# Context rows of a perceiver layer loaded in groups of four tiles instead of two

## The reference, cut to what matters

```python
x = x + xattn(layernorm(x), ctx_768)        # cross attention, one head, E = 512
x = x + attn(layernorm(x))                  # self attention, 16 heads, relative positions
x = x + ffn(layernorm(x))                   # ternary weights, gelu

# xattn, the part that the change touches
x2 = layernorm(ctx_768, ln2_g, ln2_b)       # over the 384 columns of each of 16 x 1601 rows
scores = (x1 @ Wq + bq) @ (x2 @ Wk + bk).T * E ** -0.5
out = softmax(scores) @ (x2 @ Wv + bv) @ Wo + bo
```

## Time and profile before

| | us |
|---|---|
| median of 3 runs | 593.91 |
| lowest, highest | 593.52, 597.63 |
| the profiled execution | 593.65 |
| its span, first to last instruction | 591.9 |
| PE busy | 561.1 (95%) |
| DVE busy | 418.5 (71%) |
| POOL busy | 199.6 (34%) |
| ACT busy | 216.8 (37%) |

### The profile page before, as it was taken

How to read it: one execution, slowest core, us unless ns; L and a number is a source line. 1 busy time by engine, 2 the same in 40 slices (tenths; PEclk the granted TensorE clock), 3 DMA queues, 4 the chain that set the end, 5 groups by cost and what they waited for, 6 DMA issues and landing times.

```text
span 591.9 us, 13163 instructions
## 1 busy us (share of the span) xinstructions
PE 561.1 (95%) x5237; PEld 352.9 (60%) x5237; DVE 418.5 (71%) x1026; ACT 216.8 (37%) x513; POOL 199.6 (34%) x259
## 2 busy tenths in 40 slices
PE   8999979999999999989996899999999999999797
PEld 7654444545455454534784675957759587595654
DVE  3987579999999999846868762926639265492743
ACT  0321142546455542413123361524516245152502
POOL 0324549899989987840000100101001010010010
PEclk9999999999999999999996999999999999999999
DMA  7990689999999999937743203030120401203000
GB/s 280 374 366 3 251 297 380 343 324 316 394 368 394 360 368 384 378 113 260 266 107 102 78 19 91 19 109 20 56 52 20 107 21 72 54 3 107 20 18 19
DMA packets 58973, 108.26 MB, mean 183 GB/s; under 512 B 19984, under 2 KB 22560, under 8 KB 56864
## 3 DMA queue, kind: packets, MB, share of 16 engines
q1 hardware_dynamic: 58912, 107.41, 52.3%
HBM read 96.91 MB, written 10.49 MB: 181 GB/s over the span
## 4 chain that ended last, share of the span: by engine, by line
PE 62%; DVE 17%; DMA 8%; SPq 5%; issue 4%; POOL 3%; ACT 2%; DVEq 0%; POOLq 0%
PE u_ps L1056 9%; DVE area L1206 6%; PE u_ps L915 6%; PE bank L1033 5%; PE max_ps L1033 5%; PE s_ps L889 4%; PE max_ps L961 4%; PE bank L1079 4%; PE bank L1102 4%; PE bank L961 4%; DMA area<-in_ctx_dram 4%; PE bank L945 3%; DMA area<-in_L_xattn_Wo_dram 3%; DVE area L1215 2%; DVE area L1210 2%
## 5 line engine op out<-in xcount | busy, mean ns | idle before, releaser
L499 POOL TENSOR_SCALAR area<-area 128x384 f32<-128x384 f32 (+1 forms) x160 | 106.8, 680 | 10.3 <-POOL area L492 10.3
L1206 DVE BATCH_NORM_STATS2 area<-area 128x6 f32<-128x384 f32 (+1 forms) x208 | 104.0, 542 | 6.9 <-DMA area<-in_ctx_dram 6.8
L492 POOL TENSOR_TENSOR area<-area,minus_half 128x4 f32<-128x4 f32 (+1 forms) x56 | 60.3, 1077 | 51.1 <-DVE area L1215 49.7
L915 PE MATMUL u_ps<-area,yT_all 128*64 128x384 f32 (+1 forms) x416 | 75.9, 496 | 0.0
L545 POOL TENSOR_TENSOR area<-area,minus_half 128x1 f32<-128x1 f32 x8 | 4.4, 550 | 184.9 <-DVE area L1487 184.9
L889 PE MATMUL s_ps<-area 128*64 128x512 f32 x288 | 66.0, 593 | 0.0
L1056 PE MATMUL u_ps<-area 128*128 128x512 f16 x256 | 60.1, 379 | 0.0
L915 PEld LDWEIGHTS u_ps<-area,yT_all 128*64 128x64 f32 (+1 forms) x416 | 26.3, 136 | 29.0 <-issue 27.9
L889 PEld LDWEIGHTS s_ps<-area 128*64 128x64 f32 x288 | 20.4, 137 | 36.5 <-issue 35.5
L714 ACT CAST area<-max_ps 128x512 f16<-128x512 f32 x8 | 4.7, 586 | 97.3 <-PE max_ps L1112 97.3
L1056 PEld LDWEIGHTS u_ps<-area 128*128 128x128 f16 x256 | 24.4, 98 | 25.1 <-issue 0.6
(11 more groups left out here) (187 smaller groups left out, 1041.0 us busy)
## 6 DMA issues: line engine op xcount, KB each, us to landing
area<-in_ctx_dram SPq DMA_DIRECT2D x96, 384.0 KB, 7.1
area<-in_ctx_turned_dram SPq DMA_DIRECT2D x32, 768.0 KB, 8.2
area<-in_L_ffn_W_turned_dram SPq DMA_DIRECT2D x16, 1024.0 KB, 8.9
skew<-area SPq DMA_DIRECT2D x8, 1024.0 KB, 4.0
area<-skew SPq DMA_DIRECT2D x16, 256.0 KB, 4.4
x_sb<-in_x_dram SPq DMA_DIRECT2D x8, 256.0 KB, 8.5
out_dram<-area SPq DMA_DIRECT2D x8, 256.0 KB, 2.0
area<-in_ctx_dram SPq DMA_DIRECT2D x16, 97.5 KB
```

What stands on the lines that cost most here:

```text
L492: pool.tensor_tensor(rs[b][:, sl], ve[b][:, sl], minus_half[:, 0:n], ALU.pow).then_inc(s["rstd_ready"], 1)
L499: pool.tensor_scalar(raw[b][0:m, u, j, :], raw[b][0:m, u, j, :], negmu[b][0:m, i:i + 1], rs[b][0:m, i:i + 1], ALU.add, ALU.mult).then_inc( ...
L915: ins = pe.matmul(u_ps[u * L:(u + 1) * L, 0:DC], pT[0:m, j % NSLOT, u * L:(u + 1) * L], raw[b][0:m, u, j, :], start=(j == 0), stop=(j == N ...
L1206: dve.bn_stats(st[b][0:m, stat_at(u, j), :], raw[b][0:m, u, j, :]).then_inc(s["key_stats_done"], 1)
```

## The change

From pair 2 on, `load_next` issues nothing at an even k below 6. At k = 1, 3 and 5 it waits for four tiles of pair p - 2 (the last of them is tile 2k + 1) and loads four tiles, 2k - 2 to 2k + 1, with one DMA of 768 KB for each sequence. The tail tile is loaded as before, at k = 6. `stats` waits for the group of four at j = 0, 4 and 8, and for the tail at j = 12. Pairs 0 and 1 are loaded and waited for as before, and the other DMAs keep their places in SP's order. Each group of four counts on the semaphore of its odd k.

```diff
             def load_next(p, k):
 
-                sp.wait_ge(s["tile_weighted"], NJ * (p - 2) + min(2 * k + 2, NJ))
-                load_pair(p, k)
+                b = p % 2
+                if k == NL - 1:
+                    sp.wait_ge(s["tile_weighted"], NJ * (p - 1))
+                    load_pair(p, k)
+                elif k % 2:
+                    sp.wait_ge(s["tile_weighted"], NJ * (p - 2) + 2 * k + 2)
+                    for u in range(2):
+                        full = ctx_in[2 * p + u, 0:FT * P, :].rearrange("(p j) d -> p j d", j=FT)
+                        sp.dma_start(raw[b][:, u, 2 * k - 2:2 * k + 2, :], full[:, 2 * k - 2:2 * k + 2, :]).then_inc(raw_loaded[b][k], 16)
...
-                if j % 2 == 0:
+                if j % 2 == 0 and (p < 2 or j == FT):
                     dve.wait_ge(raw_loaded[b][j // 2], 32 * (p // 2 + 1))
+                elif j % 4 == 0:
+                    dve.wait_ge(raw_loaded[b][j // 2 + 1], 32 * (p // 2 + 1))
```

## The result

The changed kernel takes 610.42 us (median of 4 runs, 607.85 to 613.61), the kernel before beside it 595.00 (4 runs). The ratio is 1.0257, 95% interval 1.0193 to 1.0321: slower by 15 us, where the forecast was 6.4 and its range 595.0 to 607.5. The profiled execution has a span of 606.1 us against 591.9.

A forecast was written before the change was run, and what follows sets the result against it. With PE, DVE, POOL and DMA level, the prediction added 1.6 us (pair 2), 4.0 (tiles 8 to 11 of pairs 3 to 6) and 0.8 (pair 7): +6.4 on 593.65 gives 600.0, range 595 to 607.5.

The forecast's parts named there:

- What bounds the kernel: In one pair's pass PE, DVE, POOL and DMA run level; relieving one gains nothing, an added wait has little room.
- Tiles 4 to 7: Margin from issue to need 7.3 us against 6.4 to load: cost 0, or about 1 behind a weight piece.
- Pair 2: First group lands 3.6 to 4.6 us late, 1.4 hidden by POOL's addition: cost 1.6 us, ends 0.5 and 3.
- Tiles 8 to 11: Pairs 3 to 6: 1.4 us of wait less 0.5 of room in POOL, taken as 1.0 a pair, 4.0 us.
- Tiles 0 to 3 of pairs 3 to 6: DVE stops 2.0 to 3.1 us before tile 0, hidden behind POOL's bias addition: cost 0.
- the cover: POOL's bias addition holds DVE at line 1215 for 2.70 us instead of 0.2 anyway, hiding the wait before tile 0.
- Pair 7: Four tiles of DVE work follow the last landing instead of two; 0.8 us counted for the group's late landing.
- the covers fail: Rival, chance 0.17: rows come 8 to 10 us after issue, 2.0 us more in each of five pairs, 610.
- Longer packets: Rival, chance 0.07 (under 593): grouped loads move at 426 GB/s instead of 396, gaining 5.0 us, 588.6.
- the packets stay as they are: Rival, inside the forecast's 0.50: longer rows are cut as before, each of 18 groups costs 0.3 us more, 602.
- 25 us of waits: Sign: DVE's waits for context rows grow from 6.8 us to some 25.
- one microsecond a pass: Sign: the passes of pairs 3 to 6 are longer by about 1 us each in PE's sums.

The follow-up runs named there:

- from_pair3: The changed kernel, but pair 2 is still loaded by twos: 608.03 us, ratio 1.0221 to the kernel before.
- g2_only: The kernel before, with only tiles 8 to 11 loaded as one group from pair 2 on: 604.88 us, ratio 1.0156.
- g0_only: The kernel before, with only tiles 0 to 3 loaded as one group from pair 2 on: 602.48 us, ratio 1.0123.
- small_weights: The changed kernel with four feed-forward weight pieces of pairs 4 and 5 loaded by a quarter: 608.32 us, ratio 1.0213 to the kernel before.
- to_pair6: The changed kernel, but pair 7 is again loaded by twos: 606.38 us, ratio 1.0197 to the kernel before.
- g1_only: The kernel before, with only tiles 4 to 7 loaded as one group from pair 2 on: 594.71 us, ratio 1.0000.
- tiles4_7_weights_last: The kernel before, with two attention weights moved behind the last context loads and only tiles 4 to 7 loaded as a group: 592.15 us, ratio 0.9943.
- coarse_wait: The kernel before, loads by twos and as early, but DVE waits for four tiles at a time in pairs 2 to 7: 604.29 us, ratio 1.0157.

## Why the prediction was wrong

**What bounds the kernel** held. PE, DVE and POOL run level, and the waits on DVE came through: its waits for rows grew from 6.8 to 28.6 us, and PE's waits for POOL from 4.0 to 15.0.

**Tiles 4 to 7** held: 0 predicted, ratio 1.0000 alone.

**Pair 2** held: 1.6 predicted, 2.6 - 1.0 = 1.6 in the table, about 2 by `from_pair3`. The wait was 3.94, within 3.6 to 4.6.

**Two steps failed: the wait before tile 8 was priced too low, and the wait before tile 0 was put at nothing.** Alone, the groups of tiles 8 to 11 cost 9.3 us (`g2_only`) where the prediction's terms for them come to 4.8, and those of tiles 0 to 3 cost 7.3 us (`g0_only`) where its terms come to 1.6. The two steps, in this order:

**Tiles 8 to 11.** The prediction took 1.4 us of wait, less 0.5 of room in POOL, for four pairs, and counted 4.0. Three parts of it were off. The group took 6.7 to 7.6 us from issue to use and not 6.4, so that the waits were 1.73, 1.54, 2.54 and 1.63 in pairs 3 to 6. The same wait in pair 2, 1.38, was left out. And the 0.5 us of room did not show: between the third and the seventh pair's issue the waits before tile 8 in `g2_only` add up to 2.76 + 2.83 + 1.06 + 2.35 = 9.0 us. Less the 2.05 us that DVE waited in these passes before, and with the 1.9 us by which the bias additions held it longer (11.3 instead of 9.4), that gives 8.8 us, and the passes are 8.5 us longer than before. POOL had that gap before its power, but DVE, which does the rest of the pass in order, had none.

**Tiles 0 to 3 of pairs 3 to 6.** The size of the wait was off, the cover was there. The prediction worked out 2.0 to 3.1 us from pair 4 and applied it to all. Pair 4 was right by itself (7.7 us from issue to use against 6.4 to 7.5), but in pairs 5 and 6 the group took 10.4 and 9.4 us, because more than the turned chunk stood in the queue: the weight pieces issued at 169.50 and 198.44 landed 9.6 and 10.1 us later, after the groups' own issues at 178.73 and 207.72. `small_weights` shows that this is what made them late. The waits of 4.29 and 2.35 us were longer than the cover there, which was 2.73 and 1.62 us before. The cover worked: line 1215 held DVE for 2.37, 2.70, 2.73 and 1.62 us in pairs 3 to 6 before, 9.4 in all, and line 1224 for 0.78, 1.26, 0.17 and 0.34 after, 2.6 in all.

With this the four passes can be added up from DVE's side: waits of 9.96 before tile 0 (pairs 3 to 6) and 7.19 before tile 8 (pairs 2 to 5), less 2.05 that it waited there before, less 9.4 - 2.6 = 6.8 of cover, gives 8.3 us. Measured are 8.9. The prediction had 3.0 for them, the tiles 8 of pairs 3 to 5. Of the 8.3, tile 8 gives 6.0 (7.19 less 1.19 that DVE waited before the tail tile of pair 5) and tile 0 gives 2.3 (9.96 less 0.86 before tile 2 of pair 6, less 6.8).

**Pair 7** was too small as well. It was right that four tiles of work would follow the last group. But the group landed 9.9 us after its issue, at 264.1. The prediction had named the late issue and priced it at 0.8; the weight and the turned chunk ahead of the group it did not reckon. The wait of 5.16 before tile 8 replaced 2.52 and 1.64; 2.5 us were added after pair 7's first issue, and `to_pair6` puts the pair at about 3.6. The prediction had 0.8, and 1.0 for pair 6's tile 8.

**The rival "the covers fail"** gave 610, and that is where the time came out, but not by its mechanism. Rows 8 to 10 us after the issue did come, in pairs 5 and 6. But it had 2 us uncovered before each tile 0, where the four passes show 2.3 in all, and most of the time came from tile 8, which it left at the forecast's price. **"Longer packets"** gain nothing, by `g1_only` and `tiles4_7_weights_last`, and "the packets stay as they are" is excluded by the packet counts. Of the signs given in advance, 25 us of waits (28.6), the shrinking line 1224 and no wait before tile 4 were right; one microsecond a pass was not (1.8, 1.8, 3.4 and 1.9). A sign of being wrong that it had named came up as well: more than 2 us of new idle time of PE in a pass, 2.8 in the third of the four passes and 2.1 in the fourth.

The rule of the Trainium skill (DMA: Bandwidth & Descriptors, section Bandwidth) that DMAs be batched to 1 MiB and more does not help here: going from 384 to 768 KB costs nothing where it can be hidden (ratio 1.0000) and brings nothing. The figures of that section, and the fit that the prediction worked out 11.6 and 7.6 us from, are given there for DMAs issued from GpSimd; the loads here are issued by SP.

What stays open: why `coarse_wait` costs 9 us, more than its waits less the cover give. In the four passes the waits are 11.7 us; less 2.1 that were there before and 7.1 of cover they give 2.5, where 3.4 are measured. Pair 2 adds 1.4 us and the end of the stage 1.1, together 5.9, which is within the expectation. Of the 9.5 us by which its span is longer, 1.9 stand there before pair 2 is touched (the turned chunk in front of pair 2's first group is issued at 92.86 before and at 94.72), and 1.7 come after the stage, where no context is loaded. No run shows where these come from. Other profiles have such parts too: up to 2.2 us in front of pair 2, and 335.0 to 338.1 us from the tail tile to the end. A difference of one or two microseconds between two single profiles is therefore laid to a change only where it lies inside the stage.

## What to carry to other kernels

For a transfer into a buffer that is freed piece by piece, compare two intervals: from the freeing of the last piece to the need of the first, and from issue to the landing of the last byte with everything that stands ahead in the queue. Here 7.3 us of margin made a group of four tiles free, 4.5 and 5.0 us made it cost 7 and 9 us over six pairs; the larger margin cost more, because there no other hold-up covered the wait. Take the second interval from the pass with the fullest queue, and count no idle gap of one engine as room when another engine does its work in order beside it. Where a stage ends on the queue, look for transfers that nobody needs yet and put them last: two weights moved gave 0.6%, more than any size of transfer did.

## What the runs showed of the hardware that was not expected

Of the two DMAs of a group, issued 0.4 us apart, the second landed 1.8 us or more after the first, and a transfer issued behind them can land almost with it: in `g0_only` the second DMA of pair 4's group, issued at 151.65, landed at 160.15, and the first of the next two, issued at 152.55, at 160.28. This group was thus as late as if part of the next load were ahead of it: it landed about 5 us after the chunk in front of it, where 1.57 MB at the 396 GB/s of the earlier trace rows would take 4.0 (an estimate), and where the same group in the changed kernel, with only a weight piece issued behind it, took 3.8. DVE's small `TENSOR_SCALAR` of four columns takes 0.17 us alone and up to 2.8 us while POOL adds two 128x512 tiles, whereas a pair of `bn_stats` that ran beside the same addition (at 160.30 in the changed kernel, within POOL's 160.27 to 162.77) took its usual 0.99 us.
